# Two experts of a pair on the two partition halves: one product, one bias column and one weight row per pair

## The chip, the cores and the metric

The kernel runs on one core of a Trainium2 chip. The metric is the time on the device in microseconds (us), as the median of several runs. The core has a matrix engine (TensorE, PE in the profile; PEld is its weight load), VectorE (DVE), ScalarE (ACT), GpSimd (POOL) and a queue on SyncE (SP) that issues most DMAs.

## What is computed

The input is 16 images of 64 channels and 16x16 pixels. Three stages follow one another: a graph-like convolution over nodes, a selective state-space layer (a scan over the tokens), and a mixture of eight experts of which each token uses two. The change lies in the last one:

```python
logits = xt @ Wr + br
probs = jax.nn.softmax(logits, axis=-1)
top_p, top_idx = jax.lax.top_k(probs, TOP_K)
weights = top_p / top_p.sum(axis=-1, keepdims=True)
xn = (xt - mu) * jax.lax.rsqrt(var + LN_EPS)
xe = xn[None, :, :] * ln_g[:, None, :] + ln_b[:, None, :]
h = jax.nn.gelu(jnp.einsum('end,edh->enh', xe, W1) + b1[:, None, :], approximate=False)
y = jnp.einsum('enh,ehd->end', h, W2) + b2[:, None, :]
y_tok = jnp.transpose(y, (1, 0, 2))
sel = jnp.take_along_axis(y_tok, top_idx[:, :, None], axis=1)
out = (weights[:, :, None] * sel).sum(axis=1)
```

Here D = 64 channels, 8 experts, hidden width 256. All arithmetic is fp32; the products with W1 and the weight rows use f32r, a faster reading of fp32 data, with W1 split into a high and a low part.

## The kernel before

**Tiling.** The 16 images are worked on in G = 8 groups of two, image g and image g + 8. A tensor of 64 channels keeps one image on partitions 0 to 63 and the other on 64 to 127, with 256 columns (pixels); a tensor of 128 partitions has T = 512 columns, the pixels of both images. The matrix engine's results lie in P, eight banks of 512 fp32 columns: XD, XA, XB, XC, YS are banks 3 to 7.

**Loop.** After a prologue (the convolution) every engine runs its own program over bodies i = 0 to 7, written out by hand, and waits on semaphores for the others. Body i does the scan of group i, the preparation of groups i + 1 and i + 2, and the router and experts of group i - 1 (`prev`). Behind body 7 the experts of group 7 follow by themselves. So there are eight expert passes, seven of them beside a scan.

**A body on TensorE** (`body` in the tensor block): out-projection of the previous group (`pe_po`), spreading products of the scan's step sizes (`pe_spread`), layernorm products, router; then the experts by `pe_pair`; behind them the projections of group i + 2 (`pe_projz`, `pe_projg`), the last f2, the products B (`pe_b`) and dt (`pe_dtz`), and four sums over the scan's states (`pe_sum`), which need GpSimd's product with C of every scan slot.

**A body on VectorE:** eight scan slots, each a product (line 762) and a scan (line 769) on 128x1024 elements. Between slots stand the gate of the previous group (`dve_gate`, which needs the last sum), the layernorm products, the router's small steps, and the experts' products in pairs.

**Experts.** For expert e and hidden half k (r = 2e + k) `pe_f1` multiplies 128 columns of W1 (high, then low part) with the normed tokens X2: 512 columns, all 128 output partitions, line 1178 and 1179. ScalarE makes hb from it by GELU. `pe_f2` multiplies W2 (128 rows, 64 output columns) with hb and accumulates k = 0 and 1. It issues two matmuls, one per image:

```python
for h in range(2):
    last = pe.matmul(P[64 * h:64 * h + 64, (XC, XD)[pair % 2], HW * (e % 2):HW * (e % 2) + HW], W2s[:, e, k, :],
                     hb[:, r % 4, HW * h:HW * h + HW], start=(k == 0), stop=(k == KC - 1))
```

`pe_pair(p)` issues f1 of expert p and then f2 of expert p - 1; this is called a step below. After steps 2 to 5 `pe_wb` spreads the token weights of two experts over the partitions, by a matmul each with the selection matrix selW and the transposed weights wT (`pe_wt`), and ScalarE copies them to wbs. VectorE forms (f2 + b2) * weight for each expert (`dve_expert`, line 860) into one of four buffers mes, and GpSimd adds it to accs (`pool_acc`, line 359), beginning with the residual t1. SP writes accs to the output. Fillers without a use (`pe_warm`) stand in some gaps.

## Time and profile before

| what | us |
|---|---|
| median of 3 runs | 400.85 (400.56 to 401.72) |
| the profiled execution | 402.59 |
| its span in the trace | 400.9 |
| TensorE busy | 337.8 |
| VectorE busy | 330.0 |
| ScalarE busy | 280.1 |
| GpSimd busy | 265.9 |

The span is one execution as the hardware profiler recorded it. Busy time is the union of an engine's instructions, so instructions that overlap count once. The body of the loop takes 38.7 us in the middle of the program. An fp32 matmul stands in the trace as two records, a f32r one as one; the end of a matmul record is modelled, so a distance between starts says more than a duration. In the rows `[0.58 <-POOL hs L347]` means that the engine was idle 0.58 us before the row, and that GpSimd's write of hs ended it. `128*64` is the shape of the weights, rows by columns.

### The profile page before, as it was taken

The numbers are of one execution on the slowest core, as the hardware profiler recorded it, in microseconds if no ns is written. First come the engines' busy times: TensorE is split into PE (matmuls) and PEld (weight loads), VectorE is DVE, ScalarE is ACT, GpSimd is POOL, SyncE is SP. The second block draws the span as 40 slices with busy tenths as digits, with TensorE's granted clock in tenths as the row PEclk, the third lists the DMA queues.
The fourth block names the chain that finished last, engine by engine and source line by source line (L and its number), as shares of the span: only waits on it lengthen the run. The fifth ranks groups of instructions, "written<-read, shape, count | busy, mean of one in ns | idle before, by whom it ended". The sixth has DMA issues, their size and how long they took to land. (4 is left out here: it accounts for less than half of the span.)

```text
span 400.9 us, 5477 instructions
## 1 busy us (share of the span) xinstructions
PE 337.8 (84%) x1658; PEld 183.1 (46%) x1658; DVE 330.0 (82%) x454; ACT 280.1 (70%) x458; POOL 265.9 (66%) x270
## 2 busy tenths in 40 slices
PE   0597896677899889989998898899889877999794
PEld 0484445333455345444544453455245425555452
DVE  2774457997899999999999999999999988994411
ACT  1002667488968997898799869987987757761472
POOL 8706112986579966994899589858985994692122
PEclk9996999588999999998999999999989986999899
DMA  8771079899899698659975897589758960000000
GB/s 196 211 146 19 0 191 222 214 222 227 206 229 217 149 213 205 155 147 212 206 165 133 199 234 164 137 191 222 166 150 194 222 141 1 2 0 15 1 0 13
DMA packets 21236, 59.52 MB, mean 148 GB/s; under 512 B 4924, under 2 KB 13272, under 8 KB 15320
## 3 DMA queue, kind: packets, MB, share of 16 engines
q1 hardware_dynamic: 20040, 58.34, 63.4%
q10 hardware_dynamic: 1168, 0.84, 0.9%
q8 instruction: 13, 0.21, 0.2%
q14 instruction: 15, 0.12, 0.1%
HBM read 53.93 MB, written 5.24 MB: 148 GB/s over the span
## 5 line engine op out<-in xcount | busy, mean ns | idle before, releaser
L347 POOL TENSOR_TENSOR hs<-hs,Cs 128x1024 f32<-128x1024 f32 x63 | 149.3, 2373 | 42.8 <-DVE hs L769 42.2
L769 DVE TENSOR_TENSOR_SCAN hs<-av,P 128x1024 f32<-128x1024 f32 x64 | 146.3, 2286 | 4.7 <-PE P L1056 1.3
L635 ACT ACTIVATE hb<-P,b1c 128x512 f32<-128x512 f32 x128 | 81.5, 683 | 18.6 <-PE P L1179 16.3
L762 DVE SCALAR_TENSOR_TENSOR P<-P,bbcol,ub 128x1024 f32<-128x1024 f32 x62 | 79.7, 1285 | 2.4 <-DMA ub<-u_scratch 1.1
L1192 PE MATMUL P<-hb,W2s 128*64 128x256 f32 x512 | 69.3, 394 | 0.0
L1178 PE MATMUL P<-X,W1H 128*128 128x512 f32 x128 | 60.1, 469 | 5.6 <-ACT hb L635 4.4
L1179 PE MATMUL P<-X,W1L 128*128 128x512 f32 x128 | 52.6, 411 | 0.0
L578 ACT ACTIVATE av<-P,Aneg 128x510 f32<-128x510 f32 x68 | 44.1, 686 | 10.9 <-PE P L1131 6.9
L359 POOL TENSOR_TENSOR accs<-accs,mes 128x256 f32<-128x256 f32 x56 | 40.9, 730 | 14.1 <-DVE mes L860 9.5
L1192 PEld LDWEIGHTS P<-hb,W2s 128*64 128x64 f32 x512 | 31.6, 137 | 31.0 <-issue 21.1
L860 DVE SCALAR_TENSOR_TENSOR mes<-P,cols,wbs 128x256 f32<-128x256 f32 x64 | 27.3, 467 | 16.9 <-PE P L1192 9.6
L1131 PE MATMUL P<-D,selD 128*128 128x512 f32 x64 | 35.1, 573 | 6.7 <-ACT av L578 4.2
L578 ACT ACTIVATE av<-av,Aneg 128x510 f32<-128x510 f32 x60 | 38.2, 707 | 0.1
L1178 PEld LDWEIGHTS P<-X,W1H 128*128 128x128 f32 x128 | 25.1, 196 | 28.3 <-ACT hb L635 17.0
L1056 PE MATMUL P<-hs,selS 128*32 128x512 f32 x256 | 30.8, 598 | 4.3 <-POOL hs L347 4.3
L628 ACT ACTIVATE wbs<-P 128x512 f32<-128x512 f32 x32 | 19.1, 598 | 20.8 <-PE P L1166 20.8
L1179 PEld LDWEIGHTS P<-X,W1L 128*128 128x128 f32 x128 | 25.5, 200 | 2.8
L1208 PE MATMUL P<-W1H 128*128 128x512 f32 x53 | 19.1, 468 | 4.7 <-POOL X L372 4.7
L1131 PEld LDWEIGHTS P<-D,selD 128*128 128x128 f32 x64 | 12.8, 207 | 20.8 <-issue 20.6
L1056 PEld LDWEIGHTS P<-hs,selS 128*32 128x32 f32 x256 | 6.7, 109 | 26.3 <-POOL hs L347 15.1
L1166 PE MATMUL P<-wT,selW 32*128 32x256 f32 x64 | 16.1, 330 | 0.0
L364 POOL TENSOR_TENSOR D<-dts,D 64x512 fp32r<-64x512 f32 x8 | 10.1, 1266 | 7.5 <-ACT D L561 6.7
(191 smaller groups left out, 478.8 us busy)
## 6 DMA issues: line engine op xcount, KB each, us to landing
ub<-u_scratch SPq DMA_DIRECT2D x31, 1024.0 KB, 10.8
av<-dt_scratch SPq DMA_DIRECT2D x15, 1024.0 KB, 7.4
dt_scratch<-dts SPq DMA_DIRECT2D x7, 256.0 KB, 2.8
u_scratch<-rl SPq DMA_DIRECT2D x7, 256.0 KB, 2.8
av<-in_L_conv_Wr SPq DMA_DIRECT2D x2, 576.0 KB, 6.9
av<-in_L_conv_Wl SPq DMA_DIRECT2D x2, 576.0 KB, 7.7
res<-in_x SPq DMA_DIRECT2D x4, 256.0 KB, 4.5
hb<-in_L_ffn_W SPq DMA_DIRECT2D x2, 512.0 KB, 6.4
```

Of the source, the lines that this page charges most:

```text
L347: gp.tensor_tensor(hs[:, at, :, :], hs[:, at, :, :], rep(Cs[:, p, :], 1, 2), ALU.mult).then_inc(S["cm"], 1)
L359: gp.tensor_tensor(acc[:, p, :], prev, mes[:, e % 4, :], ALU.add).then_inc(S["acc"], 1)
L578: a_.activation(steps, dt_of, ACT.Exp, scale=Aneg[:, m:m + 1]).then_inc(S["aexp"], 1)
L635: a_.activation(hb[:, r % 4, :], P[:, (XA, XB)[r % 2], :], ACT.Gelu, bias=b1c[:, r:r + 1]).then_inc(S["gl"], 1)
L762: v.scalar_tensor_tensor(out=ring, in0=rep(P[:, BB, :], 1, 2), scalar=bbcol[:, 0:1], in1=ub[:, 2 * n:2 * n + 2, :], op0=ALU.add, op1=ALU.m ...
L769: v.tensor_tensor_scan(hs[:, (SLOTS * g + n) % RING].rearrange("p a t -> p (a t)"), av[:, 2 * n:2 * n + 2, :].rearrange("p a t -> p (a t)" ...
L860: v.scalar_tensor_tensor(out=mes[:, e % 4, :], in0=P[:, (XC, XD)[e // 2 % 2], HW * (e % 2):HW * (e % 2) + HW], scalar=cols[:, R["b2"] + e: ...
L1056: last = pe.matmul(P[32 * q:32 * q + 32, YS, :], selS[:, k, :], hs[:, (SLOTS * g + n) % RING, q % 2, :], start=(k == 0), stop=(k == 3))
L1131: pe.matmul(P[:, (YS, XA)[m % 2], :], selD[:, m - BY_PE[0], :], D2[:, :], start=True, stop=True).then_inc(S["dt_pe"], 1)
L1178: pe.matmul(P[:, bank, :], W1H[:, e, 128 * k:128 * k + 128], X2[:, :], start=True, stop=False)
L1179: pe.matmul(P[:, bank, :], W1L[:, e, 128 * k:128 * k + 128], X2[:, :], start=False, stop=True).then_inc(S["f1"], 1)
L1192: last = pe.matmul(P[64 * h:64 * h + 64, (XC, XD)[pair % 2], HW * (e % 2):HW * (e % 2) + HW], W2s[:, e, k, :], hb[:, r % 4, HW * h:HW * h ...
```

## The change

Now the two halves of the partitions hold two experts of a pair instead of two images.

- f2: one matmul of 512 columns (both images) for each r. Expert 2j writes partitions 0 to 63, expert 2j + 1 partitions 64 to 127 of the same bank.
- The token weights are transposed for each image apart (four transposes of 16 rows), wT is 16 x 512, and one matmul of 512 columns spreads the weights of a pair. b2 is one column per pair.
- VectorE forms one product of 128x512 for each pair. mes has two buffers of 512 columns.
- GpSimd adds the four pairs with three additions of 512 columns into accs. TensorE then adds the two halves by a matmul with foldm (two identities, `pe_fold`), one body later, behind f1 of expert 0; ScalarE copies the result out (`act_folded`), and GpSimd adds it to t1 (`pool_out`). For the last group TensorE accumulates the fourth pair in the fold itself, and VectorE adds the result to t1.
- SP writes t1 instead of accs, one body later, between the loads of chunk 0 and 1.

The diff, cut to its core:

```diff
@@ -115,7 +116,8 @@
         gsel = sb("gsel", [128, NBLK])
         mask8 = sb("mask8", [128, BLK])
         selS = sb("selS", [128, 4, 32])
-        selW = sb("selW", [32, EXP, 128], f32r)
+        selW = sb("selW", [2 * EXP, PAIRS, 128], f32r)
+        foldm = sb("foldm", [128, 64])
         rank = sb("rank", [128, 4, EXP])
         selD = sb("selD", [128, len(BY_PE), 128], f32r)
         D2 = sb("D2", [128, T], f32r)
...
@@ -172,11 +174,12 @@
         rt = sb("rt", [128, 12, 4, EXP])
         rv = sb("rv", [128, 8, 4])
         vv = sb("vv", [128, 2, 2, 2, EXP])
-        wT = sb("wT", [32, HW], f32r)
+        wT = sb("wT", [2 * EXP, T], f32r)
         wbs = sb("wbs", [128, EXP, HW])
         hb = sb("hb", [128, 4, T])
-        mes = sb("mes", [128, 4, HW])
-        acc = sb("accs", [128, 2, HW])
+        mes = sb("mes", [128, 2, T])
+        acc = sb("accs", [128, T])
+        folded = sb("folded", [128, HW])
 
 
         def within(buf, at, shape):
...
@@ -257,6 +266,8 @@
             if g == 0:
                 sp_.wait_ge(S["res_ready"], 4)
             for c in range(CHUNKS):
+                if c == 1 and g >= 3:
+                    sp_out(sp_, g - 3, (g - 3) % 2)
                 since(sp_, "scan", SLOTS * (g - 1) + 2 * c + 2)
                 if g == 0 and c == 0:
                     continue
...
@@ -347,16 +352,22 @@
             gp.tensor_tensor(hs[:, at, :, :], hs[:, at, :, :],
                              rep(Cs[:, p, :], 1, 2), ALU.mult).then_inc(S["cm"], 1)
 
-        def pool_acc(eng, g, p, e):
-
-            eng.wait_ge(S["me"], EXP * g + e + 1)
-            if e == 0:
-                since(eng, "out_sem", 32 * g)
-                prev = t1[:, p, :]
+        def pool_acc(eng, g, j):
+
+            eng.wait_ge(S["me"], PAIRS * g + j + 1)
+            if j == 1:
+                since(eng, "fold", g)
+                prev = mes[:, 0, :]
             else:
-                eng.wait_ge(S["acc"], EXP * g + e)
-                prev = acc[:, p, :]
-            gp.tensor_tensor(acc[:, p, :], prev, mes[:, e % 4, :], ALU.add).then_inc(S["acc"], 1)
+                eng.wait_ge(S["acc"], 3 * g + j - 1)
+                prev = acc[:, :]
+            gp.tensor_tensor(acc[:, :], prev, mes[:, j % 2, :], ALU.add).then_inc(S["acc"], 1)
+
+        def pool_out(eng, g):
+
+            eng.wait_ge(S["ev"], g + 1)
+            eng.wait_ge(S["cen2"], g + 1)
+            gp.tensor_tensor(t1[:, g % 2, :], t1[:, g % 2, :], folded[:, :], ALU.add).then_inc(S["fin"], 1)
 
         def pool_dlo(eng, g):
 
...
@@ -482,34 +493,36 @@
                     pool_x2(eng, prev)
                     pool_router(eng, prev)
                 pool_slot(eng, i, p, 2)
+                if prev:
+                    pool_out(eng, prev - 1)
                 pool_slot(eng, i, p, 3)
                 pool_slot(eng, i, p, 4)
-                weighted(0)
                 pool_slot(eng, i, p, 5)
-                weighted(2)
+                weighted(1)
                 if nxt is not None:
                     eng.wait_ge(S["cm"], SLOTS * i + 6)
                     if prev is not None:
-                        eng.wait_ge(S["acc"], EXP * prev + 4)
+                        eng.wait_ge(S["acc"], 3 * prev + 1)
                     pool_dlo(eng, nxt)
                     eng.wait_ge(S["dlo"], nxt + 1)
                 pool_slot(eng, i, p, 6)
                 if nxt is not None and i > 0:
                     pool_restart(eng, nxt, 0)
                     pool_restart(eng, nxt, 1)
-                weighted(4)
+                weighted(2)
                 if nxt is not None:
                     pool_slot(eng, i, p, 7)
                 if nxt is not None and i == 0:
                     pool_restart(eng, nxt, 0)
                     pool_restart(eng, nxt, 1)
-                weighted(6)
+                weighted(3)
 
             for i in range(G):
                 body(i, i % 2, i + 1 if i + 1 < G else None, i + 2 if i + 2 < G else None, i - 1 if i > 0 else None)
             pool_router(eng, G - 1)
-            for e in range(EXP):
-                pool_acc(eng, G - 1, 1, e)
+            pool_out(eng, G - 2)
+            for j in (1, 2):
+                pool_acc(eng, G - 1, j)
 
 
         def act_lnA1(eng, g, bank=XD):
...
@@ -617,15 +630,21 @@
             a_.activation(chances, rt[:, 1], ACT.Exp).then_inc(S["ex"], 1)
 
         def act_wt(eng, g):
-            eng.wait_ge(S["wtr"], 2 * (g + 1))
-            since(eng, "wb_mm", EXP * g)
-            a_.activation(wT[:, :], P[0:32, XD, 0:HW], ACT.Copy).then_inc(S["wtc"], 1)
+            eng.wait_ge(S["wtr"], 4 * (g + 1))
+            since(eng, "wb_mm", PAIRS * g)
+            a_.activation(wT[:, :], P[0:2 * EXP, XD, :], ACT.Copy).then_inc(S["wtc"], 1)
 
         def act_wb(eng, g, r):
-            eng.wait_ge(S["wb_mm"], EXP * g + 2 * r + 2)
+            eng.wait_ge(S["wb_mm"], PAIRS * g + r + 1)
             if r == 0:
-                since(eng, "me", EXP * g)
-            a_.activation(wbs[:, 2 * r:2 * r + 2, :].rearrange("p e f -> p (e f)"), P[:, YS, :], ACT.Copy).then_inc(S["wb"], 1)
+                since(eng, "me", PAIRS * g)
+            a_.activation(rows_w[:, r, :], P[:, YS, :], ACT.Copy).then_inc(S["wb"], 1)
+
+        def act_folded(eng, g):
+
+            eng.wait_ge(S["fold"], g + 1)
+            since(eng, "fin", g)
+            a_.activation(folded[:, :], P[:, YS, 0:HW], ACT.Copy).then_inc(S["ev"], 1)
 
         def act_gelu(eng, g, p):
 
...
@@ -689,6 +708,8 @@
                         act_gelu(eng, prev, n)
                         if n == 0 and nxt is not None:
                             act_dhi(eng, nxt)
+                        if n == 0 and prev > 0:
+                            act_folded(eng, prev - 1)
                         if n == 1:
                             act_wt(eng, prev)
                         if n in range(2, 6):
...
@@ -851,15 +875,13 @@
             eng.wait_ge(S["ms2"], g + 1)
             v.tensor_tensor(rt[:, 8], rt[:, 7], bc(3), ALU.is_equal).then_inc(S["o2"], 1)
 
-        def dve_expert(eng, g, e):
-
-            if e % 2 == 0:
-                eng.wait_ge(S["f2"], EXP * KC * g + 2 * KC * (e // 2 + 1))
-                eng.wait_ge(S["wb"], EXP // 2 * g + e // 2 + 1)
-            since(eng, "acc", EXP * g + max(e - 3, 0))
-            v.scalar_tensor_tensor(out=mes[:, e % 4, :], in0=P[:, (XC, XD)[e // 2 % 2], HW * (e % 2):HW * (e % 2) + HW],
-                                   scalar=cols[:, R["b2"] + e:R["b2"] + e + 1], in1=wbs[:, e, :],
-                                   op0=ALU.add, op1=ALU.mult).then_inc(S["me"], 1)
+        def dve_expert(eng, g, j):
+
+            eng.wait_ge(S["f2"], EXP * KC * g + 2 * KC * (j + 1))
+            eng.wait_ge(S["wb"], PAIRS * g + j + 1)
+            since(eng, "acc", 3 * g + (j >= 2))
+            v.scalar_tensor_tensor(out=mes[:, j % 2, :], in0=P[:, (XC, XD)[j % 2], :], scalar=cols[:, R["b2"] + j:R["b2"] + j + 1],
+                                   in1=rows_w[:, j, :], op0=ALU.add, op1=ALU.mult).then_inc(S["me"], 1)
 
         @block.vector
         def _(eng):
...
@@ -1040,8 +1061,11 @@
             v.tensor_tensor(X2[64:128, :], xnt2[:, :], X2[0:64, :], ALU.subtract).then_inc(S["xl2"], 1)
             dve_router1(eng, G - 1)
             dve_router2(eng, G - 1)
-            for e in range(EXP):
-                dve_expert(eng, G - 1, e)
+            for j in range(PAIRS):
+                dve_expert(eng, G - 1, j)
+            eng.wait_ge(S["fold"], G)
+            eng.wait_ge(S["fin"], G - 1)
+            v.tensor_tensor(t1[:, (G - 1) % 2, :], P[:, YS, 0:HW], t1[:, (G - 1) % 2, :], ALU.add).then_inc(S["fin"], 1)
 
 
         def pe_sum(eng, g, k):
...
@@ -1152,19 +1176,38 @@
         def pe_wt(eng, g):
             eng.wait_ge(S["vlo"], g + 1)
             eng.wait_ge(S["xn1"], so_far(g, 4))
-            since(eng, "me", EXP * g)
-            for q in range(2):
-                pe.transpose(P[0:32, XD, 128 * q:128 * q + 128], vv[:, q].rearrange("p h r e -> p (h r e)"), ident[:, :]).then_inc(S["wtr"], 1)
+            since(eng, "me", PAIRS * g)
+            for h in range(2):
+                for q in range(2):
+                    at = HW * h + 128 * q
+                    pe.transpose(P[0:2 * EXP, XD, at:at + 128], vv[:, q, h].rearrange("p r e -> p (r e)"), ident[:, :]).then_inc(S["wtr"], 1)
 
         def pe_wb(eng, g, r):
 
             if r == 0:
                 eng.wait_ge(S["wtc"], g + 1)
+                since(eng, "ev", g)
             else:
-                eng.wait_ge(S["wb"], EXP // 2 * g + r)
-            for e in (2 * r, 2 * r + 1):
-                pe.matmul(P[:, YS, HW * (e % 2):HW * (e % 2) + HW], selW[:, e, :], wT[:, :],
-                          start=True, stop=True).then_inc(S["wb_mm"], 1)
+                eng.wait_ge(S["wb"], PAIRS * g + r)
+            pe.matmul(P[:, YS, :], selW[:, r, :], wT[:, :], start=True, stop=True).then_inc(S["wb_mm"], 1)
+
+        def pe_fold(eng, g):
+
+            eng.wait_ge(S["acc"], 3 * g + 3)
+            for h in range(2):
+                last = pe.matmul(P[64 * h:64 * h + 64, YS, 0:HW], foldm[:, :], acc[:, HW * h:HW * h + HW], start=True, stop=True)
+            last.then_inc(S["fold"], 1)
+
+        def pe_fold_last(eng, g):
+
+            eng.wait_ge(S["acc"], 3 * g + 2)
+            eng.wait_ge(S["wb"], PAIRS * (g + 1))
+            for h in range(2):
+                pe.matmul(P[64 * h:64 * h + 64, YS, 0:HW], foldm[:, :], acc[:, HW * h:HW * h + HW], start=True, stop=False)
+            eng.wait_ge(S["me"], PAIRS * (g + 1))
+            for h in range(2):
+                last = pe.matmul(P[64 * h:64 * h + 64, YS, 0:HW], foldm[:, :], mes[:, 1, HW * h:HW * h + HW], start=False, stop=True)
+            last.then_inc(S["fold"], 1)
 
         def pe_f1(eng, g, r):
             e, k = r // KC, r % KC
...
@@ -1187,11 +1230,10 @@
             if r == 2 * KC:
                 eng.wait_ge(S["wtc"], g + 1)
             if r % (2 * KC) == 0 and pair >= 2:
-                eng.wait_ge(S["me"], EXP * g + 2 * (pair - 1))
-            for h in range(2):
-                last = pe.matmul(P[64 * h:64 * h + 64, (XC, XD)[pair % 2], HW * (e % 2):HW * (e % 2) + HW], W2s[:, e, k, :],
-                                 hb[:, r % 4, HW * h:HW * h + HW], start=(k == 0), stop=(k == KC - 1))
-            last.then_inc(S["f2"], 1)
+                eng.wait_ge(S["me"], PAIRS * g + pair - 1)
+            at = 64 * (e % 2)
+            pe.matmul(P[at:at + 64, (XC, XD)[pair % 2], :], W2s[:, e, k, :], hb[:, r % 4, :],
+                      start=(k == 0), stop=(k == KC - 1)).then_inc(S["f2"], 1)
 
         def pe_pair(eng, g, p):
 
...
@@ -1362,6 +1404,8 @@
                     eng.wait_ge(S["xl2"], prev + 1)
                     pe_warm(eng, 2, XB)
                     pe_pair(eng, prev, 0)
+                    if prev > 0:
+                        pe_fold(eng, prev - 1)
                     pe_f1(eng, prev, 2)
                     pe_f1(eng, prev, 3)
                     pe_wt(eng, prev)
...
@@ -1412,6 +1458,7 @@
                 pe_wb(eng, G - 1, n - 2)
             for n in range(6, 9):
                 pe_pair(eng, G - 1, n)
+            pe_fold_last(eng, G - 1)
 
 
 _INS = [('x', 'x'), ('L0_conv_W1', 'cW1'), ('L0_conv_b1', 'cb1'), ('L0_conv_Wl', 'Wl'), ('L0_conv_bl', 'bl'),
```

On TensorE, in a body, behind f1 of expert 1, there stand before: transposes, f2 of expert 0, f1 of expert 2, f2 of expert 1, weight rows of pair 0 (line numbers are those of each kernel; P is the bank memory, hb the GELU's result).

```order
L1179 MATMUL P<-X,W1L 128x512
L1157 MATMUL P<-ident,vv 32x128 x2
L1192 MATMUL P<-hb,W2s 64x256 x4
L1178 MATMUL P<-X,W1H 128x512
L1179 MATMUL P<-X,W1L 128x512
L1178 MATMUL P<-X,W1H 128x512
L1179 MATMUL P<-X,W1L 128x512
L1192 MATMUL P<-hb,W2s 64x256 x4
L1166 MATMUL P<-wT,selW 128x256 x2
```

And now:

```order
L1183 MATMUL P<-ident,vv 16x128 x4
L1235 MATMUL P<-hb,W2s 64x512 x2
L1221 MATMUL P<-X,W1H 128x512
L1222 MATMUL P<-X,W1L 128x512
L1221 MATMUL P<-X,W1H 128x512
L1222 MATMUL P<-X,W1L 128x512
L1235 MATMUL P<-hb,W2s 64x512 x2
L1192 MATMUL P<-wT,selW 128x512
```

Each f2 burst has two matmuls of 512 columns instead of four of 256, the weight rows one instead of two; there are four transposes.

A little ahead of that, from f1 of expert 0 on, before:

```order
L1178 MATMUL P<-X,W1H 128x512
L1179 MATMUL P<-X,W1L 128x512
L1178 MATMUL P<-X,W1H 128x512
L1179 MATMUL P<-X,W1L 128x512
L1178 MATMUL P<-X,W1H 128x512
L1179 MATMUL P<-X,W1L 128x512
L1157 MATMUL P<-ident,vv 32x128 x2
```

And now:

```order
L1221 MATMUL P<-X,W1H 128x512
L1222 MATMUL P<-X,W1L 128x512
L1198 MATMUL P<-accs,foldm 64x256 x2
L1221 MATMUL P<-X,W1H 128x512
L1222 MATMUL P<-X,W1L 128x512
L1221 MATMUL P<-X,W1H 128x512
L1222 MATMUL P<-X,W1L 128x512
L1183 MATMUL P<-ident,vv 16x128 x4
```

The fold (accs by foldm) stands between f1 of expert 0 and f1 of expert 1.

On VectorE, the end of a body, from the third pair's products to the gate of the group, before:

```order
L860 SCALAR_TENSOR_TENSOR mes<-P,cols,wbs 128x256 x2
L762 SCALAR_TENSOR_TENSOR P<-P,bbcol,ub 128x1024
L769 SCALAR_TENSOR_TENSOR hs<-av,P 128x1024
L860 SCALAR_TENSOR_TENSOR mes<-P,cols,wbs 128x256 x2
L762 SCALAR_TENSOR_TENSOR P<-P,bbcol,ub 128x1024
L769 SCALAR_TENSOR_TENSOR hs<-av,P 128x1024
L790 TENSOR_TENSOR ygs<-P,sg 128x512
```

And now:

```order
L883 SCALAR_TENSOR_TENSOR mes<-P,cols,wbs 128x512
L785 SCALAR_TENSOR_TENSOR P<-P,bbcol,ub 128x1024
L792 SCALAR_TENSOR_TENSOR hs<-av,P 128x1024
L883 SCALAR_TENSOR_TENSOR mes<-P,cols,wbs 128x512
L785 SCALAR_TENSOR_TENSOR P<-P,bbcol,ub 128x1024
L792 SCALAR_TENSOR_TENSOR hs<-av,P 128x1024
L813 TENSOR_TENSOR ygs<-P,sg 128x512
```

The products stand at the same places between the scan slots, one where there were two.

## Rows read from the trace of the kernel before

**Rows 1.** The page, busy microseconds, share of the span and instructions.
```profile
PE 337.8 (84%) x1658; PEld 183.1 (46%) x1658; DVE 330.0 (82%) x454; ACT 280.1 (70%) x458; POOL 265.9 (66%) x270
```

**Rows 2.** Table by stretches, body 4: length; busy PE, PEld, DVE, ACT, POOL; clock; DMA.
```profile
210.26:248.99 38.73, 35.23 (x182) 18.11 (x182) 37.29 (x47) 33.90 (x58) 30.92 (x28) 1.00 0.79 180
```

**Rows 3.** Timeline, front part of body 4: start, length, engine, line, operation.
```profile
210.26 1.06 PE L1056 MATMUL P<-hs,selS 128*32 128x512 f32 x8 [0.26 <-POOL hs L347]
...
211.39 0.69 DVE L790 TENSOR_TENSOR ygs<-P,sg 128x512 f32<-128x512 f32 x1 [0.18 <-PE P L1056]
...
216.62 0.41 ACT L597 ACTIVATE rqs<-rqs 128x256 f32<-128x256 f32 x1
...
217.10 0.86 DVE L807 TENSOR_TENSOR xnt<-P,rqs 64x256 f32<-64x256 f32 x2
...
219.55 1.27 POOL L372 TENSOR_TENSOR X<-xnt,X 64x512 fp32r<-64x512 f32 x1 [0.27 <-DVE X L815]
...
221.84 0.47 PE L1178 MATMUL P<-X,W1H 128*128 128x512 f32 x1 [0.23 <-ACT av L578]
```

**Rows 4.** The same view, TensorE alone, expert steps of body 4.
```profile
223.75 0.50 PE L1178 MATMUL P<-X,W1H 128*128 128x512 f32 x1 [0.74 <-ACT hb L635]
...
229.91 1.08 PE L1192 MATMUL P<-hb,W2s 128*64 128x256 f32 x8
...
230.93 0.51 PE L1166 MATMUL P<-wT,selW 32*128 32x256 f32 x2
...
231.36 0.50 PE L1178 MATMUL P<-X,W1H 128*128 128x512 f32 x1
...
232.49 1.08 PE L1192 MATMUL P<-hb,W2s 128*64 128x256 f32 x8
```

**Rows 5.** The same view, last sums of bodies 4 and 6, out-projection.
```profile
248.99 1.07 PE L1056 MATMUL P<-hs,selS 128*32 128x512 f32 x8 [0.58 <-POOL hs L347]
...
250.87 0.65 PE L1110 MATMUL P<-ygs,Wouts 128*64 128x256 f32 x4 [0.81 <-DVE ygs L790]
...
326.21 1.06 PE L1056 MATMUL P<-hs,selS 128*32 128x512 f32 x8 [1.68 <-POOL hs L347]
```

**Rows 6.** The same view cut at 225.15 to 225.35 us, TensorE alone.
```profile
224.90 0.38 PE L1157 MATMUL P<-ident,vv 128*32 128x128 f32 x2
225.20 0.44 PE L1192 MATMUL P<-hb,W2s 128*64 128x256 f32 x2
```

**Rows 7.** Chain of waits: start, length, piece.
```profile
357.25 1.88 PE P L1192 x16
...
378.62 1.60 PE P L1192 x8
```

**Rows 8.** Timeline, TensorE, end of body 4: B product, first of the sums.
```profile
243.72 1.12 PE L1095 MATMUL P<-xc,Wrep 128*128 128x512 f32 x2
...
245.63 2.78 PE L1056 MATMUL P<-hs,selS 128*32 128x512 f32 x24
```

**Rows 9.** The page, costliest groups and groups by form: count, busy, mean ns, idle.
```profile
L628 ACT ACTIVATE wbs<-P 128x512 f32<-128x512 f32 x32 | 19.1, 598 | 20.8 <-PE P L1166 20.8
...
L973 DVE SCALAR_TENSOR_TENSOR res<-P,cols,res 128x512 f32<-128x512 f32 x4 | 2.9, 745 | 0.4 <-PE P L1280 0.4
```

**Rows 10.** Timeline, tail of the program, VectorE and GpSimd.
```profile
395.74 0.88 DVE L860 SCALAR_TENSOR_TENSOR mes<-P,cols,wbs 128x256 f32<-128x256 f32 x2 [2.14 <-PE P L1192]
...
396.31 1.58 POOL L359 TENSOR_TENSOR accs<-accs,mes 128x256 f32<-128x256 f32 x2 [1.41 <-DVE mes L860]
```

**Rows 11.** Timeline, body 4: a scan slot of VectorE, ScalarE behind the dt product.
```profile
237.79 1.28 DVE L762 SCALAR_TENSOR_TENSOR P<-P,bbcol,ub 128x1024 f32<-128x1024 f32 x1
...
239.11 2.29 DVE L769 TENSOR_TENSOR_SCAN hs<-av,P 128x1024 f32<-128x1024 f32 x1
...
246.05 0.67 ACT L542 ACTIVATE sp<-P,cols 128x512 f32<-128x512 f32 x1
...
248.04 3.76 ACT L578 ACTIVATE av<-av,Aneg 128x510 f32<-128x510 f32 x6
```

69 lines of the change are left out of this document (37 added, 32 removed).

## The prediction

> **What bounds the kernel now.** I read the page's busy shares first: TensorE 84%, VectorE 82% [rows 1]. Neither stands out, so the average decides nothing. Then the table by stretches, cut at the last sum of each loop body. A middle body (i = 4) takes 38.73 us, of which TensorE is busy 35.23 and VectorE 37.29, at a granted clock of 1.00, the 2.4 GHz level [rows 2]. Both are nearly full, so I followed the hand-over between them in the timeline.
>
> A body has two parts. In the front one TensorE waits on a chain of other engines: the last sum ends at 211.32 (210.26 + 1.06), VectorE gates (ygs, 211.39), runs a scan slot and the layernorm products, GpSimd writes the low half of X (219.55), and only then the expert products start, at 221.84 [rows 3]. More work elsewhere on TensorE does not change these 10.5 us. In the back part TensorE runs expert steps, projections and sums with almost no gap: the burst of f2, the weight row and f1 follow one another at once, and one expert step lasts 2.58 us (229.91 to 232.49) [rows 4]. The slack that is left is the wait ahead of the body's last sum: 0.58 us in bodies 1, 2, 4 and 5, 0.26 in body 3, 1.68 in body 6, none in body 7, 4.3 us in all [rows 3, 5]. So what is added to TensorE's back part lengthens the body, less that slack.
>
> **Part 1, f2 (the second expert product).** Before, each r issues two matmuls of 256 columns, one per image of the group, to partitions 0 to 63 and 64 to 127. Each fp32 matmul leaves two records. A narrow cut of the timeline shows two records of f2 that start at 225.20 and are both over 0.44 us later [rows 6], and the eight records of a step take 1.02 us to the next instruction's start [rows 4]: at 0.44 one after another they would take 3.5. The two halves run side by side. The double burst at the end of body 7 has eight records more and takes 1.88 [rows 7], so a pair of records passes every (1.88 - 1.02) / 4 = 0.215 us. A burst is 4 x 0.215 = 0.86, plus 0.16 for the change of shape.
>
> Afterwards both matmuls of an expert (k = 0 and k = 1) go to the same 64 partitions, and the other expert of the pair comes a step later, behind f1. Nothing stands beside them any more. Each has 512 columns. A record of a 512-column fp32 matmul takes about 0.43: the B and dt products have two records each and take 1.91 together (243.72 to 245.63) [rows 8], 0.96 each, that is 2 x 0.43 and 0.1 around them. A step's f2 becomes 4 x 0.43 + 0.16 = 1.87 instead of 1.02: +0.85 us. With 8 groups of 8 experts, **64 x 0.85 = +54.4 us**, on the path. Where no projection stands between experts 6 and 7 (bodies 6 and 7 and the last group), the first record of expert 7 may overlap the last one of expert 6: 3 x 0.43, **-1.3 us**.
>
> The trace holds no lone 64-wide fp32 matmul. Its record is bounded by 0.215 (if the pace belonged to the narrow shape) and 0.43 (the 128-wide one). I take 0.43, because the pairs start together.
>
> The Trainium skill, TensorEngine Tiling, section Instruction Overhead, states about 60 cycles for each matmul on this chip, whatever its size. By that rule the 128 matmuls fewer in f2 would give back 128 x 25 ns = 3.2 us, an estimate from that page, and the time would be 449.3. The row of the double burst speaks against it: eight further records add 0.86 us, which is their columns alone.
>
> **Part 2, the weight rows.** One matmul of 512 columns replaces two of 256. The two take 0.43 us from start to start (230.93 to 231.36). f1's four 512-column matmuls of the same type take 1.13 together (231.36 to 232.49), 0.28 each with their shape change shared [rows 4]. Bounds 0.28 and 0.43. I take 0.43, no gain, since the columns are the same and the shape change is not shared; the low end would be 32 x 0.15 = 4.8 us less. Four transposes stand where two stood; two take 0.30 from start to start with the shape change [rows 6]. Two more cost 0.1 to 0.3, I take 0.2: **8 x 0.2 = +1.6 us**. ScalarE's copy of wT gets 512 columns, about 0.60 as the copy of a weight row has it [rows 9]. The first f2 burst that waits for it stands behind two others, so it is covered.
>
> **Part 3, the fold.** Two half matmuls of 256 columns, as in the out-projection (0.65 us) [rows 5], stand behind f1 of expert 0. There TensorE is idle 0.74 us, until the first GELU is out [rows 4]. The fold fits: 0. Without that cover it is 8 x 0.6 = 4.8 us. The accumulator that it reads was finished a body earlier. ScalarE's copy of the fold stands behind two GELUs and GpSimd's last addition behind slot 2, where the next scan comes only 3.6 us later (237.79 to 241.40 is one slot) [rows 11]. On SP's queue the output DMA moves ahead of the loads of chunk 1, which are wanted a body later. All nothing.
>
> **Part 4, VectorE and GpSimd.** Two products of 256 take 0.88 us together, one of 512 about 0.75 (the residual of line 973) [rows 9, 10]: with the gaps 0.1 to 0.2 less each, some 0.5 a body. GpSimd has four pairs of additions at 1.58 us [rows 10]; three of 512 and one of 256 take their place, some 1.5 a body less. TensorE sets the body now, so this pays nothing.
>
> **What is late next.** In body 4 everything from the last f2 on moves by 6.8 + 0.2 = 7.0 us. Without the 0.58 the last sum would end at 250.05 + 7.0 - 0.58 = 256.5. VectorE's slot 0 of the next body needs the B product, which ends at 243.72 + 0.96 + 7.0 = 251.7, and takes 3.6: 255.3, in time. ScalarE's chain behind the dt product (from 246.05 to 248.04 + 3.76 = 251.80) is 5.75 long [rows 11]. It can now start with the end of the dt product, at 245.63 + 7.0 = 252.6, and ends at 258.4, 1.9 after the sum; before it was 1.75. Further on xnt follows ScalarE's rqs at once (217.03 and 217.10) [rows 3], so these 0.15 are lost. Of the 0.58 about 0.4 comes back: four times 0.4, 0.1 in body 3, and the 1.68 of body 6, which projects no further group. **-3.4 us**, between 0 and -4.3.
>
> **Part 5, the tail.** Before: products 0.88 and additions 1.58, of which one overlaps, 2.2 from the last f2 to the DMA (395.74 to 397.89) [rows 10]. After: product 0.75, fold 0.65, addition about 0.48 and three gaps, 2.0. The last group's first burst takes 1.60 instead of 1.01 [rows 7], since part of it runs at the lower clock; the longer one may pay 0.5 more. **+0.3 us**.
>
> **Sum.** 54.4 - 1.3 + 1.6 - 3.4 + 0.3 = +51.6 us. The profiled execution took 402.59 us (span 400.9), the median of the runs is 400.85, 1.74 less. 402.59 + 51.6 = 454.2, in terms of the median **452.5 us**, 13% slower.
>
> **Rivals.**
> 1. More is absorbed: all idle time ahead of the sums comes back, transposes cost 0.1, the weight row 0.28. 54.4 - 1.3 + 0.8 - 4.3 - 4.8 + 0.3 = +45.1, 446 us. For it: the other engines have slack now. Against: the front chain of rows 3 is VectorE's own work. Chance 0.13.
> 2. New stalls. VectorE takes the products in line between scan slots. The sixth burst is out at 232.49 + 2 x 2.57 + 1.02 = 238.65 before and 6 x 0.85 + 0.2 = 5.3 later now, 243.95; VectorE is there at 241.4 (239.11 + 2.29) [rows 4, 11]. So slot 7 starts 2.5 us late. I find some 1.2 us of room ahead of the gate even so. If this stall costs 1 us more than I think and the fold is not covered, 7 x 1.6 = 11, up to 464 us. Chance 0.12.
> 3. Faster. The pace of 0.215 belongs to the 64-wide shape, and a 512-column record takes that too. The point from which it decides: a body gives back 0.38 (0.58 less the transposes) over 32 records, so from 0.227 a record on the change is slower. Below it VectorE's 0.5 a body and nothing else remains, 7 x 0.5 = 3.5 less, 397 us. For it: no lone record is to be seen. Against: pairs of equal start [rows 6], and the quarter-wide sums, eight records of 512 columns in 1.07 us [rows 5], which run in fours. Chance 0.04. Beside it: the Trainium skill, TensorEngine Tiling, section Key Properties, has tiles execute in parallel, which would leave half of the array idle under a lone one; what a lone one takes no row here shows.
> 4. The change does not do what it says: matmuls of one expert or of two overlap after all, by the queue's looking ahead. Half of part 1 would go, 425 us. Against: k = 0 and k = 1 accumulate in the same partitions, and f1 with its full width stands between experts. Chance 0.03.
>
> **How the numbers follow.** The forecast has 0.68. Its upper bound is the fold uncovered and nothing given back, 452.5 + 4.8 + 3.4 = 461; the lower one is rival 1's 446. This leaves out rivals 3 and 4 and the far end of rival 2, under 0.2. A measurement of this kernel tells about 0.3% from no change. Faster by more than that: 0.03; within it: 0.02; slower: 0.95.
>
> **What the next profile would show.** f2 with 256 records instead of 512, each about 0.43 us or more apart, 1.87 us for a step. Bodies of about 45.4 us instead of 38.7. No idle time ahead of the last sum. VectorE waiting for f2 ahead of its products and for the sum ahead of the gate, its share near 72%. The fold in the gap behind expert 0's f1. I am wrong if f2's records stand 0.22 apart, if a step's f2 is far from 1.87, or if VectorE or ScalarE still ends last in the bodies.

## The result and the profile after

The changed kernel takes 448.77 us (median of 4 runs, 446.44 to 449.71), the kernel before 400.71 beside it: ratio 1.119, 95% interval 1.114 to 1.124. The forecast was 452.5 us with a range of 446 to 461.

From the page of the changed kernel: the busy shares that answer to [rows 1], the chain that ended last by source line, and two costly groups of the expert stage, f2 (now line 1235) and VectorE's products (now line 883). The columns of a group are count, busy us, mean ns of one, idle us before it and what ended most of that.

```profile
span 447.9 us, 4935 instructions
...
PE 394.7 (88%) x1422; PEld 181.5 (41%) x1422; DVE 328.7 (73%) x423; ACT 284.2 (63%) x465; POOL 252.9 (56%) x237
...
PE P L1235 25%; PE P L1221 10%; PE P L1222 7%; PE P L1080 5%; ACT av L591 4%; PE P L1192 3%; PE P L1250 2%; PE P L1268 2%; PE P L1155 2%; PE P L1119 2%; PE P L1100 2%; DVE hs L792 2%; PE P L1114 2%; DVE P L785 1%; PE P L1109 1%
...
L1235 PE MATMUL P<-hb,W2s 128*64 128x512 f32 x256 | 118.9, 605 | 0.0
...
L883 DVE SCALAR_TENSOR_TENSOR mes<-P,cols,wbs 128x512 f32<-128x512 f32 x32 | 23.8, 745 | 58.5 <-PE P L1235 49.7
```

There are 236 matmul records fewer, and TensorE is busy 57 us longer. f2 alone went from 69.3 us busy to 118.9 and holds a quarter of the chain that ended last. VectorE's products cost 23.8 us instead of 27.3, but in front of them it now waits 49.7 us for f2 (9.6 before).

The table by stretches, cut at the end of each body's last sum, for body 4 and then body 5 of the changed kernel. The columns are those of [rows 2]: length, busy PE, PEld, DVE, ACT, POOL, clock, DMA share, GB/s.

```profile
231.01:276.17 45.16, 42.65 (x152) 17.99 (x152) 37.32 (x42) 34.29 (x58) 29.71 (x24) 1.00 0.67 154
...
276.17:322.17 46.00, 43.88 (x152) 18.66 (x152) 37.32 (x42) 34.41 (x58) 29.65 (x24) 0.96 0.66 152
```

At the same clock body 4 went from 38.73 to 45.16 us, TensorE's busy time in it from 35.23 to 42.65, and VectorE's stayed at 37.3. The timeline of TensorE in the expert steps shows where it went (start, length, engine, line, operation), to be held beside [rows 4] and [rows 5]:

```profile
242.79 0.65 PE L1198 MATMUL P<-accs,foldm 128*64 128x256 f32 x4
243.60 0.50 PE L1221 MATMUL P<-X,W1H 128*128 128x512 f32 x1 [0.16 <-ACT hb L654]
...
244.18 0.50 PE L1221 MATMUL P<-X,W1H 128*128 128x512 f32 x1
244.52 0.40 PE L1222 MATMUL P<-X,W1L 128*128 128x512 f32 x1
244.75 0.60 PE L1183 MATMUL P<-ident,vv 128*16 128x128 f32 x4
245.29 1.93 PE L1235 MATMUL P<-hb,W2s 128*64 128x512 f32 x4
247.15 0.51 PE L1221 MATMUL P<-X,W1H 128*128 128x512 f32 x1
...
250.15 0.49 PE L1192 MATMUL P<-wT,selW 16*128 16x512 f32 x1
250.57 0.51 PE L1221 MATMUL P<-X,W1H 128*128 128x512 f32 x1
...
272.53 3.64 PE L1080 MATMUL P<-hs,selS 128*32 128x512 f32 x32
```

An f2 burst lasts from 245.29 to 247.15, 1.86 us instead of 1.02, with four records instead of eight. The weight row takes 0.42 (0.43 before). Four transposes take 0.54 (244.75 to 245.29), two took 0.30. The 32 records of the four sums now run as one block, so the idle time of [rows 5] ahead of the last sum is gone. The fold (242.79) stands in the gap that was 0.74 us long, and 0.16 of it is left.

Body by body (lengths between the ends of the last sums, before: 133.83, 172.57, 211.32, 250.05, 288.81, 327.27, 365.33):

| stretch | before | after | difference | forecast |
|---|---|---|---|---|
| start to end of body 1 | 133.83 | 140.05 | +6.2 | +6.6 |
| body 2 | 38.74 | 45.79 | +7.1 | +6.6 |
| body 3 | 38.75 | 45.17 | +6.4 | +6.9 |
| body 4 | 38.73 | 45.16 | +6.4 | +6.6 |
| body 5 | 38.76 | 46.00 | +7.2 | +6.6 |
| body 6 | 38.46 | 42.47 | +4.0 | +4.9 |
| body 7 | 38.06 | 43.21 | +5.2 | +6.6 |
| last group | 35.57 | 40.05 | +4.5 | +6.9 |
| sum | 400.9 | 447.9 | +47.0 | +51.6 |

(Rows are rounded. The forecast of a row is 7.0 us less the idle time that should come back; bodies 6, 7 and the last group have the overlap of part 1, the last group also the tail.)

### The profile page after: what moved, and what is told of

It reads as the page before. It is cut to its first block, busy times and chain, and to the rows that moved or that the text cites. A ratio compares the mean times of both kernels' runs of the same rounds, so it can differ in the third digit from the quotient of the medians.

```text
span 447.9 us, 4935 instructions
## 1 busy us (share of the span) xinstructions
PE 394.7 (88%) x1422; PEld 181.5 (41%) x1422; DVE 328.7 (73%) x423; ACT 284.2 (63%) x465; POOL 252.9 (56%) x237
## 4 chain that ended last, share of the span: by engine, by line
PE 73%; ACT 9%; DVE 8%; issue 5%; POOL 3%; DMA 1%; SPq 0%; ACTq 0%; POOLq 0%; DVEq 0%
PE P L1235 25%; PE P L1221 10%; PE P L1222 7%; PE P L1080 5%; ACT av L591 4%; PE P L1192 3%; PE P L1250 2%; PE P L1268 2%; PE P L1155 2%; PE P L1119 2%; PE P L1100 2%; DVE hs L792 2%; PE P L1114 2%; DVE P L785 1%; PE P L1109 1%
## 5 line engine op out<-in xcount | busy, mean ns | idle before, releaser
L1235 PE MATMUL P<-hb,W2s 128*64 128x512 f32 x256 | 118.9, 605 | 0.0
L883 DVE SCALAR_TENSOR_TENSOR mes<-P,cols,wbs 128x512 f32<-128x512 f32 x32 | 23.8, 745 | 58.5 <-PE P L1235 49.7
L1235 PEld LDWEIGHTS P<-hb,W2s 128*64 128x64 f32 x256 | 29.2, 136 | 57.0 <-issue 41.6
L1155 PE MATMUL P<-D,selD 128*128 128x512 f32 x64 | 33.9, 556 | 5.9 <-ACT av L591 5.1
L364 POOL TENSOR_TENSOR accs<-accs,mes 128x512 f32<-128x512 f32 x15 | 19.1, 1275 | 18.7 <-DVE mes L883 18.7
L1080 PE MATMUL P<-hs,selS 128*32 128x512 f32 x256 | 29.6, 600 | 0.0
L1250 PE MATMUL P<-W1H 128*128 128x512 f32 x53 | 18.1, 448 | 4.9 <-POOL X L383 4.9
L364 POOL TENSOR_TENSOR accs<-mes 128x512 f32<-128x512 f32 x8 | 10.1, 1267 | 12.5 <-DVE mes L883 12.5
L1192 PEld LDWEIGHTS P<-wT,selW 16*128 16x128 f32 x32 | 5.8, 181 | 26.0 <-issue 26.0
```

What stands on the lines that cost most here:

```text
L364: gp.tensor_tensor(acc[:, :], prev, mes[:, j % 2, :], ALU.add).then_inc(S["acc"], 1)
L1080: last = pe.matmul(P[32 * q:32 * q + 32, YS, :], selS[:, k, :], hs[:, (SLOTS * g + n) % RING, q % 2, :], start=(k == 0), stop=(k == 3))
L1155: pe.matmul(P[:, (YS, XA)[m % 2], :], selD[:, m - BY_PE[0], :], D2[:, :], start=True, stop=True).then_inc(S["dt_pe"], 1)
L1235: pe.matmul(P[at:at + 64, (XC, XD)[pair % 2], :], W2s[:, e, k, :], hb[:, r % 4, :], start=(k == 0), stop=(k == KC - 1)).then_inc(S["f2"], 1)
L1250: pe.matmul(P[:, bank, :], W1H[:, 0, 0:128], W1H[:, 0:2, :].rearrange("p e f -> p (e f)"), start=True, stop=True)
```

## The experiments

Of each experiment only the edit is shown; the rest of the kernel is as named.

**e1: the length of the instruction.** The changed kernel, f2 in pieces of 256 columns.

```diff
+            if k == 0:
+                return
             at = 64 * (e % 2)
-            pe.matmul(P[at:at + 64, (XC, XD)[pair % 2], :], W2s[:, e, k, :], hb[:, r % 4, :],
-                      start=(k == 0), stop=(k == KC - 1)).then_inc(S["f2"], 1)
+            for h in range(2):
+                for kk in range(KC):
+                    last = pe.matmul(P[at:at + 64, (XC, XD)[pair % 2], HW * h:HW * h + HW], W2s[:, e, kk, :],
+                                     hb[:, (r - 1 + kk) % 4, HW * h:HW * h + HW], start=(kk == 0), stop=(kk == KC - 1))
+            last.then_inc(S["f2"], KC)
```

> The changed kernel, but each f2 matmul of 512 columns is issued as two of 256 again, both into the same 64 partitions (column half 0 with k = 0 and 1, then column half 1); an expert's four matmuls follow one another once its second GELU is out. Theory (the halves of the partitions must both have work): a burst has eight records that nothing runs beside, 8 x 0.215 + 0.16 = 1.88 us, the time stays at 446 to 451 us. Rival A (the length of an instruction matters: 256 columns were fast, 512 are slow): the burst falls back to 1.02 us, the time to about 402. Rival B (each matmul has a fixed cost, 60 cycles by the Trainium skill, TensorEngine Tiling, Instruction Overhead): 128 matmuls more, 3.2 us by that estimate, a burst of 1.91 or more.

Measured: 450.44 us (one run). Its timeline, an f2 burst and the weight row behind it:

```profile
247.95 1.94 PE L1239 MATMUL P<-hb,W2s 128*64 128x256 f32 x8
249.82 0.49 PE L1192 MATMUL P<-wT,selW 16*128 16x512 f32 x1
```

The burst has the instructions of the kernel before in number and size and takes 1.87 us (247.95 to 249.82), not 1.02. Rival A falls: the length of the instruction is not what makes the burst slow; all four write the same half of the partitions, as in the changed kernel. Rival B falls too: four matmuls instead of two leave the burst at 1.87 against 1.86, and a body takes 45.2 us, as in the changed kernel. The 60 cycles of the Trainium skill (TensorEngine Tiling, Instruction Overhead) do not show when matmuls follow one another and each has 256 columns. The example that the section gives is of matmuls of 1 to 60 columns, and no run here has such short ones back to back.

**e2: the order inside a burst.** The kernel before, its four f2 matmuls grouped by image.

```diff
+            if k == 0:
+                return
             for h in range(2):
-                last = pe.matmul(P[64 * h:64 * h + 64, (XC, XD)[pair % 2], HW * (e % 2):HW * (e % 2) + HW], W2s[:, e, k, :],
-                                 hb[:, r % 4, HW * h:HW * h + HW], start=(k == 0), stop=(k == KC - 1))
-            last.then_inc(S["f2"], 1)
+                for kk in range(KC):
+                    last = pe.matmul(P[64 * h:64 * h + 64, (XC, XD)[pair % 2], HW * (e % 2):HW * (e % 2) + HW], W2s[:, e, kk, :],
+                                     hb[:, (r - 1 + kk) % 4, HW * h:HW * h + HW], start=(kk == 0), stop=(kk == KC - 1))
+            last.then_inc(S["f2"], KC)
```

> The kernel before, but the four f2 matmuls of an expert stand grouped by image: k = 0 and 1 for partitions 0 to 63, then k = 0 and 1 for partitions 64 to 127, all behind the second GELU. Theory (TensorE starts a matmul for the idle half ahead of older ones for the busy half, as the double burst of 2.24 us suggests): the second half starts one record late, a burst is 5 x 0.215 + 0.16 = 1.24 us, 64 x 0.22 = 14 us more less up to 4 of slack: 410 to 415 us. Rival (matmuls start strictly in program order): the second half can start only with the last record of the first, 7 x 0.215 + 0.16 = 1.66 us, about 437 us. Rival (no overlap at all in this order): 1.88 us, 447 us.

Measured: 401.23 us (one run), the kernel before 401.35 beside it. The first row is the view cut at 228.45 to 228.6 us, the others are whole:

```profile
228.50 0.44 PE L1195 MATMUL P<-hb,W2s 128*64 128x256 f32 x2
...
228.50 1.09 PE L1195 MATMUL P<-hb,W2s 128*64 128x256 f32 x8
229.52 0.51 PE L1166 MATMUL P<-wT,selW 32*128 32x256 f32 x2
```

None of the three expected numbers came: the burst still takes 1.02 us (228.50 to 229.52), neither 1.24 nor 1.66. Two records are under way from 228.50 on, although the first matmul for the upper half is third in the program, behind both of the lower half. The rows do not name the half of a record. But records of one half do not overlap (e1: eight of them take 1.87 us), so the two are of different halves: TensorE took the third matmul ahead of the second. It did so without the delay of one record that I had read out of the double burst of the changed kernel. That reading was wrong, and e6 settles it.

**e5: full width between the halves.** The kernel before, one half of f2 behind each f1 of a step (`pe_f2` issues both k for one image h and counts 1). This splits six of the eight experts: the two halves of expert 0 and of expert 7 still stand together.

```diff
-            if p < EXP:
-                pe_f1(eng, g, 2 * p)
-                pe_f1(eng, g, 2 * p + 1)
-            if p > 0:
-                pe_f2(eng, g, 2 * p - 2)
-                pe_f2(eng, g, 2 * p - 1)
+            for x in range(2):
+                if p < EXP:
+                    pe_f1(eng, g, 2 * p + x)
+                if p > 0:
+                    pe_f2(eng, g, 2 * p - 2 + x, x)
```

> The kernel before with the same instructions in another order: for experts 1 to 6 the two f2 matmuls of one image (k = 0 and 1, partitions 0 to 63) stand behind the first f1 of the step, those of the other image behind its second f1, so that f1 with its full width separates the halves. Theory (the halves run side by side only if nothing of full width stands between them): each half takes 4 x 0.215 + 0.16 = 1.02 us by itself, a step is about 1.1 us longer, 8 groups x 6 x 1.1 = 53 us more less up to 4 of slack: 446 to 454 us, with nothing else of the change in it. Rival (what the change lost came from the length of the instructions, the fold or the transposes): 401 to 410 us.

Measured: 454.56 us (one run), 54 more than the kernel before (400.41 beside it) and 0.6 above the range that I had given. TensorE in one step:

```profile
257.20 0.51 PE L1166 MATMUL P<-wT,selW 32*128 32x256 f32 x2
...
258.30 1.08 PE L1192 MATMUL P<-hb,W2s 128*64 128x256 f32 x4
259.31 0.50 PE L1178 MATMUL P<-X,W1H 128*128 128x512 f32 x1
...
259.97 1.08 PE L1192 MATMUL P<-hb,W2s 128*64 128x256 f32 x4
260.98 0.51 PE L1166 MATMUL P<-wT,selW 32*128 32x256 f32 x2
```

Half a burst, four records of 256 columns for one half, takes as long (1.01 us, 258.30 to 259.31) as the whole one with eight did. The step grew from 2.58 to 3.78 us (257.20 to 260.98). This is a loss as large as that of the change, with no fold, no new transposes and no pair in it: the same instructions of f2 in another order. It shows the cause in the layout of the kernel before, and e3 shows it in that of the changed one.

**e3: both experts of a pair in each burst.** The changed kernel, f2 in the order r = 0, 2, 1, 3 of a pair, a step later.

```diff
+NH = 6
+F2_ORDER = [4 * j + x for j in range(PAIRS) for x in (0, 2, 1, 3)]
+SLOT = list(range(NH))
+for _r in range(NH, EXP * KC):
+    SLOT.append(SLOT[F2_ORDER[_r - NH]])
...
-            if p > 0:
-                pe_f2(eng, g, 2 * p - 2)
-                pe_f2(eng, g, 2 * p - 1)
+            if p > 1:
+                pe_f2(eng, g, F2_ORDER[2 * p - 4])
+                pe_f2(eng, g, F2_ORDER[2 * p - 3])
```

The diff leaves out the further calls of `pe_pair` and the buffers. hb has NH buffers, the GELU of r writes hb[:, SLOT[r]]. The weighted products and their sums stay in place in wbs, so that mes and accs make room for the six buffers.

> The changed kernel, but f2 runs by pairs of experts: a step issues k = 0 of the even expert and k = 0 of the odd one, the next step k = 1 of both, so that each burst has work for both partition halves. hb has six buffers instead of four; to make room the weighted products and their sums are kept in wbs in place, mes and accs are gone. f2 starts one step later. Everything else of the change stays. Theory: single bursts take 1.02 us, the last double one 1.88; per body 8.0 us of f2 instead of 14.9. f1 of expert 2 now waits for the GELU with no f2 burst to cover it, about +1 us in a body. 398 to 405 us. Rival (the fold, the four transposes or VectorE's waiting in line make the loss): the bursts shrink, the time stays above 430 us.

Measured: 400.06 us (median of 10 runs), ratio to the kernel before 0.997 (0.994 to 0.999). Its timeline, the end of the steps and of the body:

```profile
225.07 0.50 PE L1221 MATMUL P<-X,W1H 128*128 128x512 f32 x1 [0.60 <-ACT hb L655]
...
238.66 1.08 PE L1235 MATMUL P<-hb,W2s 128*64 128x512 f32 x4
239.67 1.13 PE L1100 MATMUL P<-xnt,Wzs 128*128 128x256 f32 x4
...
241.60 1.94 PE L1235 MATMUL P<-hb,W2s 128*64 128x512 f32 x8
243.46 1.13 PE L1119 MATMUL P<-xc,Wrep 128*128 128x512 f32 x2
```

A burst of four 512-column records, two for each half, takes 1.01 us (238.66 to 239.67), the double one 1.86 (241.60 to 243.46). The f2 matmuls are those of the changed kernel; what stands beside them differs (and the buffers named above), and all of its 48 us of loss are gone. The expected stall in front of f1 of expert 2 is there, 0.60 us where I had put about 1. A body takes 38.92 (249.83 less 210.91, the out-projections), 0.2 more than before.

**e6: the double burst, in the order of the changed kernel.** As e3, but for the last pair the order is r = 12, 13, 14, 15.

```diff
-F2_ORDER = [4 * j + x for j in range(PAIRS) for x in (0, 2, 1, 3)]
+F2_ORDER = [4 * j + x for j in range(PAIRS) for x in ((0, 2, 1, 3) if j < PAIRS - 1 else (0, 1, 2, 3))]
```

> As e3_alternate, but the double burst of experts 6 and 7 stands in the order of the changed kernel (both of expert 6, then both of expert 7); unlike there, all GELUs are long out when it starts. Theory (the 2.24 us of the changed kernel's double burst are 0.38 of waiting for the GELU of expert 7 and 1.86 of full overlap; TensorE passes over older matmuls of the busy half without loss): the burst takes 1.86 us as in e3, the time 399 to 401 us. Rival (the second half starts one record late in this order): 2.3 us. Rival (strictly in order): 3 x 0.43 + 1.72 + 0.16 = 3.2 us, 1.3 us more in a body, about 409 us.

Measured: 402.02 us (one run; its first out-projection stands at 96.93 us against 94.38 in e3, so 2.5 us of it lie ahead of the expert stage, which is more than the 1 us by which it missed the expected 399 to 401). The double burst:

```profile
244.16 1.94 PE L1235 MATMUL P<-hb,W2s 128*64 128x512 f32 x8
246.03 1.12 PE L1119 MATMUL P<-xc,Wrep 128*128 128x512 f32 x2
```

It takes 1.87 us, as in e3. In program order the four records of the upper half stand behind all four of the lower one, and they run beside them with no loss. So the double burst of the changed kernel, 2.24 us (357.70 to the next product at 359.94), must have another reason for its length. Here is the changed kernel's timeline at the end of body 6. The first two rows are the same burst with the view cut at 357.75 and 358.2 us; ScalarE's GELU and the weight loads (PEld) follow:

```profile
357.70 0.64 PE L1235 MATMUL P<-hb,W2s 128*64 128x512 f32 x1
...
357.70 1.07 PE L1235 MATMUL P<-hb,W2s 128*64 128x512 f32 x3
...
357.34 1.26 ACT L654 ACTIVATE hb<-P,b1c 128x512 f32<-128x512 f32 x2 [1.74 <-PE P L1222]
...
358.08 0.24 PEld L1235 LDWEIGHTS P<-hb,W2s 128*64 128x64 f32 x3 [0.19 <-ACT hb L654]
```

At first one record is under way alone, later they come two at a time. Weight loads at 358.08 were released by a GELU of expert 7, which I take for the upper half's first: it starts 0.38 us late because its operand is 0.38 us late. 0.38 + 1.86 = 2.24.

**e7: the fold twice.** The changed kernel, `for h in (0, 1, 0, 1)` in the fold.

```diff
-            for h in range(2):
+            for h in (0, 1, 0, 1):
```

> The changed kernel with each fold (but the last group's) computed twice, with the same result. Theory (the first fold lies in TensorE's wait for the first GELU, which has some 0.16 us left): the second costs 0.58 - 0.16 = 0.4 us in each of 7 bodies, 3 us in all: 449 to 453 us, and f1 of expert 1 follows it without idle time. Rival (the fold is not covered as it stands): 0.58 us each, 4 us. Rival (ScalarE or VectorE sets the pace there): no difference.

Measured: 449.29 us (one run), against 448.77. The runs of the changed kernel spread over 3.3 us, so the time does not tell; a body does: 45.21 us (231.76 less 186.55, the out-projections), against 45.16.

```profile
242.73 1.08 PE L1198 MATMUL P<-accs,foldm 128*64 128x256 f32 x8
243.75 0.50 PE L1221 MATMUL P<-X,W1H 128*128 128x512 f32 x1
244.09 0.39 PE L1222 MATMUL P<-X,W1L 128*128 128x512 f32 x1
244.32 0.40 PE L1221 MATMUL P<-X,W1H 128*128 128x512 f32 x1
```

Two folds take 1.02 us (242.73 to 243.75). The second adds 0.44 and not 0.58, since a further fold of the same shape costs its columns alone. Of that only 0.05 reaches the length of a body; I had expected 0.4, so this step of my theory was wrong. The 0.16 ahead of f1 of expert 1 takes part of it. Another part lies one matmul further on: with a single fold the weight load of the second f1 there waits 0.28 us for ScalarE's second GELU (244.18), and that f1 takes 0.34 us from its high to its low part (244.18 to 244.52). Here there is no such wait, and the second f1 follows 0.23 after the row ahead of it (244.09 to 244.32). So ScalarE sets the pace there, as the last of the rivals had it, and a single fold costs these bodies nothing.

**e4: the fold moved.** As e3, the fold behind the transposes, where the first f2 burst stood, and its copy behind that of wT.

```diff
-                    if prev > 0:
-                        pe_fold(eng, prev - 1)
                     pe_f1(eng, prev, 2)
                     pe_f1(eng, prev, 3)
                     pe_wt(eng, prev)
+                    if prev > 0:
+                        pe_fold(eng, prev - 1)
```

> As e3_alternate, but the fold stands behind the transposes, where the first f2 burst stood, and ScalarE's copy of it behind the copy of wT, so that the GELUs of expert 1 are not delayed. Theory: the fold covers the wait that e3 opens; 1 us less in a body than e3, 395 to 399 us, faster than the kernel before, because VectorE has 0.5 and GpSimd 1.5 us less in a body and f2 one shape change less. Rival (the wait ahead of the last sum comes back in full, from VectorE's scans): 399 to 401 us, no difference to the kernel before.

Measured: 400.01 us (10 runs), ratio 0.997 (0.994 to 1.000). The theory's 395 to 399 did not come: e3's wait of 0.60 is gone, but the old one is back.

```profile
223.15 0.50 PE L1220 MATMUL P<-X,W1H 128*128 128x512 f32 x1 [0.74 <-ACT hb L655]
...
224.83 0.65 PE L1197 MATMUL P<-wbs,foldm 128*64 128x256 f32 x4
225.41 0.50 PE L1220 MATMUL P<-X,W1H 128*128 128x512 f32 x1
```

There are two gaps and one fold; wherever it stands, the other one stays open. A body takes 38.73 us, as before. The time is the rival's (399 to 401), but its reason is not: the four sums run as one block here too, with no wait ahead of the last one.

**e8: ScalarE's order.** As e3, with the GELUs of expert 1 ahead of the copies of dts and of the fold.

```diff
-                        if n == 0 and nxt is not None:
-                            act_dhi(eng, nxt)
-                        if n == 0 and prev > 0:
-                            act_folded(eng, prev - 1)
                         if n == 1:
                             act_wt(eng, prev)
+                        if n == 1 and nxt is not None:
+                            act_dhi(eng, nxt)
+                        if n == 1 and prev > 0:
+                            act_folded(eng, prev - 1)
```

> As e3_alternate, but ScalarE does the GELUs of expert 1 before its copies of dts (line 574) and of the fold. In e3 TensorE waits 0.60 us there ahead of f1 of expert 2, and the body is 38.9 us. Theory: that wait goes and the body falls to about 38.3 us, 394 to 397 us, 1% faster than the kernel before. Rival (VectorE's scans are late next, with GpSimd's product ahead of the last sum): an idle time ahead of the last sum comes back, 397 to 400 us.

Measured: 397.87 us (median of 12 runs), the kernel before 400.41 beside it, ratio 0.9945 (0.9917 to 0.9972). Stretch between two out-projections, then TensorE at the place of e3's wait, which is gone, and the four sums:

```profile
208.80:247.15 38.35, 35.75 (x153) 15.79 (x153) 36.91 (x43) 34.12 (x58) 29.71 (x24) 1.00 0.78 181
...
222.11 0.50 PE L1220 MATMUL P<-X,W1H 128*128 128x512 f32 x1
...
242.69 3.64 PE L1079 MATMUL P<-hs,selS 128*32 128x512 f32 x32
```

Bodies of 38.35 us, 0.38 shorter than before, and no idle time ahead of the last sum. The theory's body length came out; the time is 0.9 us above its range of 394 to 397. This version beats both kernels, the one before by half a percent. In such a body TensorE is busy longer than before (35.75 us against 35.23) and idle shorter (2.60 against 3.50): the gap behind expert 0's f1 holds the fold, and the wait for GpSimd ahead of the last sum is gone. That this last wait went because VectorE and GpSimd have less to do is argued, not shown. Nor does a run give the kernel before ScalarE's new order; the wait that the order removes in e3 does not exist there, since f1 of expert 2 follows the f2 burst at once.

## Why the prediction was right, point by point

**What bounds.** Right. TensorE's back part carries nearly the whole addition. The front part, from the last sum's end to the fillers ahead of f1, took 9.55 us before (211.32 to 220.87) and takes 9.71 now (231.01 to 240.72): the 0.15 that I had put down to ScalarE's decays is about that large. The trace bears out the cause. At the border of bodies 3 and 4 the chain of waits does not go through the sums at all (start, length, piece; the last row is from the timeline):

```profile
227.47 0.69 ACT sp L555
...
229.48 3.50 ACT av L591 x6
...
233.96 0.47 PE L1155 MATMUL P<-D,selD 128*128 128x512 f32 x1 [0.19 <-ACT av L591]
```

ScalarE starts when the dt product is out, does its decays (av), and TensorE waits 0.19 us for one of them ahead of its own product at 233.96, a wait that it did not have before. ScalarE's rqs starts 5.46 us after the last sum's end (236.47), 5.30 before (216.62 in [rows 3]). One of my signs of being wrong was that ScalarE still ends last in the bodies. In this place it does, by these 0.16 us and as forecast; the added length is TensorE's. At the next border (276.17) the chain goes through the sums and only then to ScalarE, so the two paths are nearly even.

**Part 1, the burst.** Right. Forecast 1.87, measured 1.86 against 1.02. e1, e3 and e5 show the reason: a burst is cheap if both halves of the partitions have work in it. The range between 0.215 and 0.43 a record is settled at 0.43, and rival 3 with it.

**Part 1, the double burst.** Here a step failed, in mechanism and size. I wrote that expert 7's first record may overlap expert 6's last, -0.43 in each of three places. This assumes that TensorE starts matmuls in program order. It does not (e2, e6): the double burst took 2.24 where 3.16 was forecast, 0.92 less at three places, 2.8 of the 4.6 us by which the sum was too high. Rival 4 had half of this, for the whole of part 1, and I argued it down with the accumulation of k = 0 and 1 and with the f1 between experts. The first argument holds inside an expert, not between two, and no f1 stands inside a double burst.

**Parts 2 and 3.** Weight row 0.42 (forecast 0.43), two more transposes 0.24 (forecast 0.2), the fold nothing in bodies 3 and 4 and in the last group, where the gap holds it. In bodies 2, 5, 6 and 7 the gap did not hold it; see the fold and the lower clock below.

**Part 4 and what is late next.** The products took 3.5 us less in all (27.3 to 23.8), 0.44 a body where 0.5 was forecast, yet VectorE's busy time in a body stayed at 37.3. From the start of a product to the next instruction it is 0.64 us now and was 0.76 (252.59 to 253.23, before 232.74 to 233.50), 0.5 for four; the five waits that VectorE now has there keep apart records that overlapped by some 0.1 each, which I take for the rest. GpSimd's fell by 1.2 a body (30.92 to 29.71), not 1.5. Neither sets the time. VectorE waits 2.57 us ahead of pair 2's product, as rival 2 worked out (2.5), and it costs nothing, as I had found. But the room was smaller than the 1.2 us that I gave. VectorE at the end of body 4:

```profile
263.94 0.75 DVE L883 SCALAR_TENSOR_TENSOR mes<-P,cols,wbs 128x512 f32<-128x512 f32 x1 [2.57 <-PE P L1235]
...
273.75 2.29 DVE L792 TENSOR_TENSOR_SCAN hs<-av,P 128x1024 f32<-128x1024 f32 x1 [0.69 <-PE P L1080]
...
276.24 0.69 DVE L813 TENSOR_TENSOR ygs<-P,sg 128x512 f32<-128x512 f32 x1 [0.19 <-PE P L1080]
```

The first scan of the next body waits for the first sum of this one (0.69 us), because the ring of states has eight slots and the sum still reads the one that the scan is to write. It ends at 276.04, the gate starts at 276.24, so 0.2 us were left. I had not listed that wait; it stands beside the path by a hair.

**Slack.** In body 4 the whole 0.58 came back ahead of the sum and 0.16 went in the front part, 0.42 net where 0.4 was forecast. With 8 x 0.84 for the bursts, 0.24 for the transposes, -0.58, 0.16 for the front part and -0.04 for the weight rows the sum is 6.50, measured 6.43. For body 6 I had counted 1.68 us of waiting and overlooked a second wait. TensorE stood 1.28 us ahead of the B product, until VectorE was done with the bank:

```profile
320.72 1.10 PE L1095 MATMUL P<-xc,Wrep 128*128 128x512 f32 x2 [1.28 <-DVE P L762]
```

Now the B product follows the double burst at once (359.94), so these 1.28 came back too. With 6 x 0.84 for the single bursts, 0.36 for the double one, 0.24 for the transposes and -1.68 the sum is 3.96, measured 4.01. That it fits without the 1.28 is luck: the fold made up for most of them.

**The fold and the lower clock.** This is a term that I had put at nothing. In bodies 2, 5, 6 and 7 of the changed kernel the f1 of expert 0 runs at the lower clock (the four matmuls stand 0.43 us apart instead of 0.23), and then no gap is left behind it. Here are the first f1 of expert 0 and of expert 1, for body 3 of the kernel before, which had the lower clock in this place, and then for body 5 of the changed kernel:

```profile
183.13 0.71 PE L1178 MATMUL P<-X,W1H 128*128 128x512 f32 x1
...
185.05 0.57 PE L1178 MATMUL P<-X,W1H 128*128 128x512 f32 x1
...
286.86 0.77 PE L1221 MATMUL P<-X,W1H 128*128 128x512 f32 x1
...
289.75 0.50 PE L1221 MATMUL P<-X,W1H 128*128 128x512 f32 x1
```

Before, the distance is 1.92 us, and 1.91 at the full clock (221.84 to 223.75): the slower f1 only used up the wait for the GELU. With the fold it is 1.91 at the full clock (241.69 to 243.60), but 2.63, 2.89, 2.90 and 2.90 in bodies 2, 5, 6 and 7. Against the same bodies before (1.91, 1.91, 1.83 and 1.84) that is 0.7 to 1.1 us each and 3.8 in all; the prediction had 0.6 for a fold without cover, and nothing in its sum. It explains why bodies 2 and 5 are 0.6 and 0.8 us longer than bodies 3 and 4.

**The rest of the difference.** For body 7 the first sum of body 6, with no slack to give back, is 5.64, and the fold adds 1.1; measured is 5.15. Its granted clock was 0.87 before and 0.96 now, and its part from the last sum to f1 went from 11.37 us to 10.44. In the last group my +0.5 for the lower clock had the wrong sign: the first burst took 1.60 before and 1.86 now, at the full clock, so 0.26 more and not 1.35, which is 1.1 us of the error. The rest of the tail came as forecast: 1.96 us from the last f2 to the DMA, where I had 2.0. So the total came within 4 us in part by luck: the double bursts (2.8), the overlooked wait of body 6 (1.3) and the last group's first burst (1.1) made the sum too high, and the fold (3.8) made it too low. The remaining 3.2 us of the 4.6 are spread over the bodies, 0.9 of them in the front part of body 7. These are readings of single profiled runs, and no run here takes the clock apart from the order.

## What to carry to other kernels

For matmuls with 64 output columns TensorE worked like two engines, one for each half of the partitions: 1.86 us for a burst with one half, 1.02 for the same work on both. Give both halves work between any two instructions of full width. To see whether they have it, count in the order listing what stands beside each half-wide matmul. The order inside such a stretch did not matter (e2, e6), the operands' arrival did (0.38 us in the changed kernel's double burst). A gap that covers an addition at the full clock may not be there when the matmuls ahead of it run at the lower one: the fold cost nothing in two bodies and 0.7 to 1.1 us in four. A layout with half of f2's instructions can still be had at no loss (e3, e8), if pairs are formed where the matmuls are issued and not only where the results lie.

## What the runs showed of the hardware that I had not expected

- TensorE started matmuls for an idle half ahead of older ones for the busy half: with four records of 512 columns in front in program order (e6) the double burst still took 1.87 us, with the experts alternating (e3) 1.86. In program order it would have been 3.2.
- A burst with work for only one half costs the same per column as a full-width fp32 matmul, 0.43 us per record of 512 columns, and 1.01 us for four records of 256 with the shape changes (e5), as much as eight for both halves (1.02).
- Splitting a 512-column matmul in two of 256 cost nothing measurable in a burst (1.87 against 1.86, e1).
